# A selective scan's running sum on GpSimd: the first state opens it, and a transfer adds the skip term in memory

## The reference, cut to what matters

```python
def step(state, inp):
    d, b, c, u = inp
    dA = jnp.exp(d[..., None] * A)
    state = state * dA + (d * u)[..., None] * b[:, None, :]
    y = jnp.einsum('bdn,bn->bd', state, c)     # sum over 16 states
    return (state, y)
_, ys = jax.lax.scan(step, state0, (dt_t, B_t, C_t, u_t))
y = jnp.moveaxis(ys, 0, 2)
y = y + D[None, :, None] * x                   # x is u, the skip term
```

## Time and profile before

| | |
|---|---|
| runs, us | 1683.97, 1689.63, 1693.1: median 1689.63 |
| the profiled execution, us | 1691.41, its span 1689.5 |
| GpSimd busy | 1247.6 us, 74% of the span |
| TensorE busy | 1436.1 us, 85% |
| VectorE busy | 1304.9 us, 77% |
| ScalarE busy | 1045.2 us, 62% |
| DMA engines, mean busy | 36.8% on the hardware queue, 117 GB/s |
| TensorE's mean granted clock | 0.922 |

### The profile page before, as it was taken

One profiled execution on the slowest core, in us unless ns is written; L12 is line 12 of the kernel. 1 busy time (PEld: TensorE's weight loads), 2 busy tenths in 40 slices (PEclk: granted clock), 3 DMA queues, 4 the chain that ended last, 5 costly groups with the idle time before them and its releaser, 6 DMA issues.

```text
span 1689.5 us, 23299 instructions
## 1 busy us (share of the span) xinstructions
PE 1436.1 (85%) x7632; PEld 1149.2 (68%) x7632; DVE 1304.9 (77%) x2375; ACT 1045.2 (62%) x2408; POOL 1247.6 (74%) x613
## 2 busy tenths in 40 slices
PE   4642489999989999989999989996478999898996
PEld 1210368887778888878888868885356777676784
DVE  3997158889988989888899888889537768577575
ACT  2885146666655666656666666666347757567574
POOL 1343139999989999989999899999748537266264
PEclk9765679999999999999999999999689999899998
DMA  4444633345454344534434624424333122132021
GB/s 161 163 151 200 206 100 106 80 139 147 134 176 119 91 128 144 184 123 122 136 93 149 206 82 125 125 75 145 121 119 96 38 89 63 35 97 69 26 69 56
DMA packets 122817, 198.23 MB, mean 117 GB/s; under 512 B 10868, under 2 KB 60536, under 8 KB 121160
## 3 DMA queue, kind: packets, MB, share of 16 engines
q1 hardware_dynamic: 122696, 196.75, 36.8%
HBM read 150.18 MB, written 46.53 MB: 116 GB/s over the span
## 4 chain that ended last, share of the span: by engine, by line
PE 40%; DVE 16%; POOL 16%; issue 11%; ACT 5%; DMA 1%; SPq 1%; POOLq 0%; DVEq 0%; ACTq 0%
PE banks L583 10%; PE banks L585 9%; PE banks L584 9%; POOL act_buf L1846 5%; POOL state L1196 4%; POOL state L1185 4%; DVE state L1111 3%; PE banks L1390 3%; PE banks L1391 2%; PE banks L1392 2%; DVE banks L1904 1%; PE banks L791 1%; DVE ow_lo L1020 1%; DVE negmax L1051 1%; PE banks L814 1%
## 5 line engine op out<-in xcount | busy, mean ns | idle before, releaser
L1196 POOL TENSOR_TENSOR state<-state,Cn 128x1024 f32<-128x1024 f32 x128 | 311.0, 2430 | 57.1 <-DVE state L1111 57.0
L1185 POOL TENSOR_TENSOR state<-dtu_sb,Bn 128x1024 f32<-128x1024 f32 x128 | 313.4, 2449 | 30.0 <-DMA Bn<-scratch_bc 16.2
L1202 POOL TENSOR_TENSOR y_sb<-y_sb,state 128x1024 f32<-128x1024 f32 x128 | 308.5, 2410 | 22.5 <-DMA y_sb<-scratch_y 12.5
L1111 DVE TENSOR_TENSOR_SCAN state<-banks,state 128x512 f32<-128x512 f32 x256 | 310.3, 1212 | 4.7 <-ACT banks L952 2.0
L1846 POOL TENSOR_TENSOR act_buf<-act_buf,wb 128x512 f32<-128x512 f32 x128 | 165.9, 1297 | 171.1 <-ACT act_buf L1746 169.1
L583 PE MATMUL banks<-x_hi,w_hi 128*128 128x512 f32 (+1 forms) x512 | 187.8, 367 | 68.7 <-DVE w_lo L1015 43.6
L952 ACT ACTIVATE banks<-dt_sb,negA 128x512 f32<-128x512 f32 x256 | 177.3, 693 | 108.4 <-DVE state L1111 107.6
L585 PE MATMUL banks<-x_hi,w_lo 128*128 128x512 f32 (+1 forms) x512 | 178.7, 349 | 0.0
L584 PE MATMUL banks<-x_lo,w_hi 128*128 128x512 f32 (+1 forms) x512 | 178.4, 349 | 0.0
L583 PEld LDWEIGHTS banks<-x_hi,w_hi 128*128 128x128 f32 x512 | 101.8, 199 | 89.0 <-issue 45.3
L1894 DVE TENSOR_TENSOR hid_lo<-banks,hid_hi 128x512 fp32r<-128x512 f32 x136 | 93.7, 689 | 54.1 <-ACT hid_hi L1758 52.0
(11 more groups left out here) (218 smaller groups left out, 4437.2 us busy)
## 6 DMA issues: line engine op xcount, KB each, us to landing
Bn<-scratch_bc SPq DMA_DIRECT2D x64, 256.0 KB, 4.0
x_hi<-scratch_xs SPq DMA_DIRECT2D x32, 512.0 KB, 5.2
x_lo<-scratch_xs SPq DMA_DIRECT2D x32, 512.0 KB, 6.3
Cn<-scratch_bc SPq DMA_DIRECT2D x64, 256.0 KB, 3.3
scratch_acc<-acc_sb SPq DMA_DIRECT2D x64, 256.0 KB, 2.1
wb<-scratch_wT SPq DMA_DIRECT2D x64, 256.0 KB, 3.3
acc_sb<-scratch_acc SPq DMA_DIRECT2D x48, 256.0 KB, 3.1
w_stage<-in_w SPq DMA_DIRECT2D x32, 256.0 KB, 3.1
```

The lines of the kernel that those rows point to most:

```text
L1111: nc.vector.tensor_tensor_scan(row, dA[:, :], row, 0.0, ALU.mult, ALU.add) \
L1185: nc.gpsimd.tensor_tensor(st[:, k % 4], dtu[:, 2 * h:2 * h + 2, :], Bn[:, state % NB, :].unsqueeze(1).broadcast_to([P, 2, T]), ALU.mult).t ...
L1196: nc.gpsimd.tensor_tensor(st[:, k % 4], st[:, k % 4], Cn[:, state % NB, :].unsqueeze(1).broadcast_to([P, 2, T]), ALU.mult).then_inc(S["gat ...
L1202: nc.gpsimd.tensor_tensor(y[:, 2 * h:2 * h + 2, :], y[:, 2 * h:2 * h + 2, :], st[:, k % 4], ALU.add).then_inc(S["piece_done"], 1)
```

## The change

For the first state of a batch (r = 0) GpSimd's product with C goes straight into y, and there is no add: this opens the sum, so y doesn't hold the skip term in SBUF any more. When a half's sum over the 16 states is finished, GpSimd itself issues a transfer (`accum_op=ALU.add`) that adds it to the skip term in memory. The loads of y and SP's stores are gone. The product that opens the next batch's half waits until that half's transfer has landed; the waits for `y_stored` and `piece_done` at the stage's end become waits for the landed transfers. `piece_done` now counts only the 120 adds that are left, and `added(k)` turns a piece's number into that count. `drive(k)` of a buffer whose last piece had no add waits for its product.

```diff
         load_stage(4)
         load_c(0)
-        load_half(y, "y", 0, 0)
         load_stage(5)
-        load_half(y, "y", 0, 1)
         load_acc(0)
...
-            if r == 0 and 0 < b < B:
-                store_y(b - 1, 0)
...
-            if r == 0 and 0 < b < B:
-                sp.wait_ge(S["y_stored"], 32 * b - 16)
-                load_half(y, "y", b, 0)
-                store_y(b - 1, 1)
...
-            if r == 0 and 0 < b < B:
-                sp.wait_ge(S["y_stored"], 32 * b)
-                load_half(y, "y", b, 1)
         for h in range(2):
-            store_y(B - 1, h)
             sp.wait_ge(S[f"acc_stored{h}"], 16 * NM // 2)
-        sp.wait_ge(S["y_stored"], 32 * B)
+            sp.wait_ge(S[f"y_added{h}"], 16 * B)
...
     def gpsimd(pool):
+        def added(k):
+
+            return k + 1 - 2 * (k // (2 * NS)) - min(k % (2 * NS) + 1, 2)
+
         def drive(k):
...
-            if k >= 4:
-                pool.wait_ge(S["piece_done"], k - 3)
+            if k >= 4 and (k - 4) // 2 % NS == 0:
+                pool.wait_ge(S["gated"], k - 3)
+            elif k >= 4:
+                pool.wait_ge(S["piece_done"], added(k - 4))
...
-            nc.gpsimd.tensor_tensor(st[:, k % 4], st[:, k % 4],
+            if r == 0:
+                if b > 0:
+                    pool.wait_ge(S[f"y_added{h}"], 16 * b)
+                to = y[:, 2 * h:2 * h + 2, :]
+            else:
+                to = st[:, k % 4]
+            nc.gpsimd.tensor_tensor(to, st[:, k % 4],
                                     Cn[:, state % NB, :].unsqueeze(1).broadcast_to([P, 2, T]),
                                     ALU.mult).then_inc(S["gated"], 1)
-            if r == 0:
-                pool.wait_ge(S[f"y_loaded{h}"], 16 * (b + 1))
-            pool.wait_ge(S["gated"], k + 1)
-            nc.gpsimd.tensor_tensor(y[:, 2 * h:2 * h + 2, :], y[:, 2 * h:2 * h + 2, :],
-                                    st[:, k % 4], ALU.add).then_inc(S["piece_done"], 1)
+            if r > 0:
+                pool.wait_ge(S["gated"], k + 1)
+                nc.gpsimd.tensor_tensor(y[:, 2 * h:2 * h + 2, :], y[:, 2 * h:2 * h + 2, :],
+                                        st[:, k % 4], ALU.add).then_inc(S["piece_done"], 1)
             if k + 3 < NDRIVE:
                 drive(k + 3)
+            if r == NS - 1:
+
+                pool.wait_ge(S["piece_done"], added(k))
+                nc.gpsimd.dma_start(d["y"][b][:, 2 * h * T:2 * (h + 1) * T], half(y, h), accum_op=ALU.add) \
+                    .then_inc(S[f"y_added{h}"], 16)
...
         sp.dma_start(rbias[:, :], d["route_b"].broadcast_to([P, NE])).then_inc(S["rows_loaded"], 16)
+        for h in range(2):
+            sp.wait_ge(A[f"y_added{h}"], 16)
         load_y(sp, 0)
...
         act.wait_ge(A["acc_done"], NM)
-        act.wait_ge(A["piece_done"], NDRIVE)
-        act.wait_ge(A["y_stored"], 32 * B)
+        for n in range(2):
+            act.wait_ge(A[f"y_added{n}"], 16 * B)
```

More of the change, by code:

```diff
@@ L572, in attend_and_scan @@
              "acc_loaded0", "acc_loaded1", "acc_stored0", "acc_stored1",
-             "dt_loaded0", "dt_loaded1", "dtu_loaded0", "dtu_loaded1", "y_loaded0", "y_loaded1", "y_stored",
+             "dt_loaded0", "dt_loaded1", "dtu_loaded0", "dtu_loaded1", "y_added0", "y_added1",
              "b_loaded0", "b_loaded1", "c_loaded0", "c_loaded1",
@@ L644, in store_acc @@
             sp.dma_start(acc_rows("acc", m), acc[:, m % 2, :]).then_inc(S[f"acc_stored{m % 2}"], 16)
-        def store_y(b, h):
-            sp.wait_ge(S["piece_done"], 2 * NS * (b + 1) - 1 + h)
-            sp.dma_start(d["y"][b][:, 2 * h * T:2 * (h + 1) * T], half(y, h)).then_inc(S["y_stored"], 16)
         load_stage(0)
```

## The result

| | median us (runs) | ratio to before, 95% interval |
|---|---|---|
| before | 1689.63 (5: 1683.97 to 1693.1) | 1 |
| changed kernel | 1677.67 (5: 1675.61 to 1688.13) | 0.9947 [0.9921, 0.9973] |
| changed kernel, measured again | 1677.34 (6: 1675.69 to 1679.08) | 0.9940 [0.9919, 0.9960] |

The ratios give 0.53% and 0.60%, so 9 to 10 us; the medians of the first comparison lie 12.0 us apart, those of the second 9.4 (1686.71 and 1677.34). The forecast was 6.7 us, 1683: the direction and the place were right, the size was too small.

What follows compares the result with a forecast made beforehand. Attention was taken to set the pace until piece 100, with GpSimd close behind, and GpSimd after it. Gains of 6.5 us in attention and 0.2 at the stage's end, 6.7 in all, took 1689.6 to 1683 us; range 1672 to 1698.

Steps and rivals of the forecast that it cites:

- An add before piece 100: GpSimd in the attention-and-scan stage: removing an add before piece 100 gains nothing by itself, behind it the full time.
- Removed adds 0: Eight GpSimd adds, 19.2 us, and 12.5 us of idle before them: 0 on the path, since GpSimd meets attention again.
- SP's queue 0: Eight loads and eight stores leave SP's queue, 7 us of issue: 0, since no engine wait ends on a transfer.
- Attention gains 6.5 us: VectorE's output-weight splits behind batch boundaries lose less on the port shared with GpSimd: 6.5 us, 4.5 to 8.
- second pairs: Second two output-weight splits on VectorE behind each boundary: free of GpSimd but for some lateness, 3.5 us gained in all.
- first pairs: First two output-weight splits on VectorE behind each boundary, 9.8 us lost: 3.0 us gained as a round number.
- d: GpSimd's issue of one transfer: at least 0.43, at most 2.4 us, taken as 1.0.
- L: Issue to landing of an add in memory: at least 3.0, at most 10.2 us, taken as 8.
- The end of the stage, 0.2: Transfers and last attention store before ScalarE is freed: last arrival about 0.2 us earlier than now.
- A: GpSimd's removed work counts in full: 23.7 us gained, 1666 us; chance 0.08.
- B: No gain on the shared port, as GpSimd's phase may meet projection-weight splits worse: 1689 us; chance 0.32.
- C: Add in memory lands late, delaying products of 33, 65, 97 and ScalarE: +14.6 us, 1704 us; chance 0.14.

Runs made afterwards that it cites:

- extras: Changed kernel plus four idle GpSimd operations, behind pieces 37, 44, 70, 76 (1682.49 us) or behind pieces 108, 112, 116, 120 (1687.34 us).
- the first profile: Profiled execution from the changed kernel's first measurement, by far the longest of its five: 1688.13 us.
- the last kernel above: Changed kernel with only the one-row value bias's split moved from VectorE to GpSimd: 1674.52 us, 0.9906 of the kernel before.
- the second profile: Profiled execution from the changed kernel measured again without edit: 1677.82 us.
- the eight operations put back: Changed kernel with early products into the state buffer again and a GpSimd fill of y for each, transfers kept: 1689.29 us, 1.0012 of the kernel before.
- the four late operations: Changed kernel plus four idle GpSimd operations behind the adds of pieces 108, 112, 116 and 120: 1687.34 us, 0.9990 of the kernel before.
- the four early ones: Changed kernel plus four idle GpSimd operations behind the adds of pieces 37, 44, 70 and 76: 1682.49 us, 0.9971 of the kernel before.
- the kernel without splits: Output and projection weights' 36 VectorE splits made memsets: 1655.32 us in the kernel before, 1645.34 us in the changed one.

## Why the forecast was right, and where it was too small

**An add before piece 100 shortens nothing by itself; one behind it counts in full.** The second half is shown (8 us of extras cost 8.3 in their stretch). The first half holds for the stretches with the extras, yet they cost 5 us in the median, most of it where the projection weights' splits stand. The rule needs the words "except through the port".

**Removed adds 0, opening product 0, SP's queue 0.** The waits for scans took up what was removed. I forecast that they grow to about 25 us; they are 26.3 and 35.2. The plain store by SP again, with its issues, changes no stretch. Piece 100 was to start some 6 us earlier: its product starts 3.8 us earlier in the first profile and 13.7 in the second. From there to the end of the last add it is 195.1 and 195.2 us, forecast 194 plus the issue.

**Attention gains 6.5 us: the term that was too small.** It measured 8.1 and 9.6 at the boundaries. The second pairs were taken at 3.5 and gave 3.8 in the first profile and 3.0 in the second. The first pairs were taken at 3.0 and gave 4.6. The step that failed is the count at the first two boundaries, "gain there about 0" at the first and 1.1 at the second; they gave 0.5 and 2.0, the third 2.1 for the 2.0 I had. I had the product of piece 33 start at 482.5, 11.75 us behind the end of piece 32's scan, and GpSimd work through until piece 35. It started 10.2 and 10.4 us behind it, so GpSimd already waits at piece 34, and only one split of each first pair meets it, at all three boundaries. In the first profile the transfer was issued 1.0 us earlier than I had counted, since the issue for the first half did not push GpSimd back, and it landed in 7.45 us instead of 8; in the second it was issued when I had counted and landed in 6.6. The count was sound for its landing time. At the first boundary of the last kernel above (the value bias on GpSimd) the product of piece 33 starts 11.8 us behind the scan, that of 34 waits for nothing, and the pair is as long as before the change:

```profile
481.77 2.39 POOL L1228 TENSOR_TENSOR state<-state,Cn 128x1024 f32<-128x1024 f32 x1
...
486.23 3.72 DVE L1023 SCALAR_TENSOR_TENSOR ow_lo<-w_stage,subln,ow_hi 128x512 fp32r<-128x512 f32 x2 [0.33 <-ACT ow_hi L853]
```

So 0.8 us of GpSimd's time, from 15.7 to 16.5 us behind the scan at the product of piece 34, decides what a first pair gives, and a single landing time was too coarse a term.

The other 1.5 us of the second profile were a term I didn't have: TensorE's granted clock at the boundary, 0.91 in the one profile of before and with the eight operations put back; 0.95 in the second profile of the changed kernel, with SP's store, with the four late operations and with the value bias on GpSimd, and at two of the three boundaries with the four early ones; but 0.90 in the first profile. That the shorter boundary raises it is likely from these and not shown. Nor was there a term for the stretches between: of the 14.1 us by which the second profile is shorter than that of before from the first scan to the last, 1.6 lie in pieces 36 to 48 and 2.6 in 80 to 96. With the eight operations put back 36 to 48 takes 84.6 us all the same, and 80 to 96 takes 121.7. So no run ties either to the removed operations, and that the total came near the forecast owes something to chance.

The Trainium skill (SBUF — State Buffer, Who interferes with whom) says that a VectorE operation with two inputs in SBUF contends with a GpSimd operation that reads SBUF, and calls the shared port pair an exclusive lock. The trace agrees, and the wait lasts until the other's instruction ends: 2.55 us for a split of 0.45, beside a GpSimd operation of 2.4.

**Issue and landing.** d was taken as 1.0 and is 0.88 us, L as 8 and is 7.3 us (5.9 to 8.7). Both were bounded by rows of before, and both sizes held. The Trainium skill's line for such a transfer (DMA: Bandwidth & Descriptors, the anatomy of one DMA) gave an estimate of 3.2 us; the measurement is more than twice that, and decides.

**The end of the stage, 0.2.** It is 0.0 to 0.1. The forecast that the last attention sum's store arrives together with the last add in memory was right in kind: that store now frees ScalarE.

**The rivals.** A (full count, 1666): refuted as the cause, since 24 us didn't come and GpSimd waits longer for scans; but removed work counts in part in the kernel without splits (7.1 us from scan to scan, where A's sum has 24). B (no gain on the port, 1689): the pairs did become shorter, in both profiles. What it said of the phase is seen, though: the mid-stage extras gave back some 5 us in the stretches of the projection weights' splits. C (late landing, 1704): refuted by the landing times and by SP's plain store; in the kernel without splits the waits for the landing did grow, by 5 us.

**What stays open.** Of the 12 us between the changed kernel and the one with eight operations put back, 8 have rows, 2.5 of them only together with a lower clock, and what decides the clock of an execution has none. No run took away the one collision that is left in each first pair without moving the split.

## What to carry to other kernels

When two engines are both over 90% busy, ask for each stretch which one waits for the other, and look for the place where that turns: before it a saving on the follower becomes idle time, behind it the saving counts in full. Then look at what the follower disturbs while it works, since a saving there can still pay through a shared port, and count every operation of the leading engine that meets it, the tiny ones too. Moving a disturbed operation to the disturbing engine frees it of the collision but puts it into that engine's queue, and who waits for its result must be known first.

## What the runs showed of the hardware

- A one-partition VectorE operation of 256 elements took 0.45 us when it started 0.13 us ahead of a GpSimd operation of 2.4 us, and 2.52 when it started 0.15 us behind one.
- An add in memory of 512 KB issued by GpSimd held the engine for 0.88 us and landed 5.9 to 8.7 us after its issue; a plain store of it, issued by SyncE, took 5.1 in the median.
- A GpSimd addition over 128 x 1024 whose two inputs are the same tile took 1.90 us, with two different tiles 2.40.
- TensorE's granted clock at the boundaries was 0.90 or 0.95 in two executions of one kernel, though TensorE was idle as long: in the 10 us from the pair on, 6.55 us busy at 0.72 in the one and 6.56 at 0.83 in the other. In pieces 48 to 64, 0.97 went with 121.7 us and 1.00 with 119.2, TensorE busy 2.2 us longer; but 121.6 us were also seen at 1.00 (80 to 96 with the four early operations). A difference of 2.5 us in one stretch needs the clock column, or a second profile, before it is laid to an edit.
